# Attention sums as columns: one-column 32-bit products in a bank of scores, with the single key's share added from a list

## What is computed

```python
def sdpa(q, k, v):
    scores = jnp.einsum('bshd,blhd->bhsl', q, k) * scale
    attn = jax.nn.softmax(scores, axis=-1)
    return jnp.einsum('bhsl,blhd->bshd', attn, v)
...
out_img = sdpa(q, k_img, v_img)
out = (out_txt + out_img).reshape(B, S, INNER)
return out @ o_w + o_b
```

## Time and profile before

| what | value |
|---|---|
| median of 3 runs | 1903.29 us (1898.18 to 1903.45) |
| the profiled execution | 1903.73 us, its span 1902.0 us |
| TensorE products, busy | 1733.7 us, 91% |
| VectorE busy | 1397.3 us, 73% |
| GpSimd busy | 1204.3 us, 63% |
| ScalarE busy | 985.9 us, 52% |
| the attention loop | about 231 to 1427 us of the span |

### The profile page before, as it was taken

The page is one execution under the profiler, slowest core; times in us unless marked ns, Lnnn a source line. Parts: engine busy times, 40 slices in busy tenths (PEclk is TensorE's granted clock), DMA queues, the critical chain, the costliest instruction groups (busy, mean ns, idle before and its releaser), DMA issues. The chain is left out here.

```text
span 1902.0 us, 30825 instructions
## 1 busy us (share of the span) xinstructions
PE 1733.7 (91%) x8731; PEld 1541.6 (81%) x8731; DVE 1397.3 (73%) x2577; ACT 985.9 (52%) x1657; POOL 1204.3 (63%) x1053
## 2 busy tenths in 40 slices
PE   7899889999999999999999999999992998699998
PEld 6677778888889889888888898898891886588887
DVE  4444587887887887978878878879772664577776
ACT  3455455565555555655655565556552563244443
POOL 1333588878878888788788798798862231133332
PEclk9999899999999999999999999999996999799999
DMA  3366554566556465554565564564436782133332
GB/s 110 127 239 232 175 164 104 114 123 137 115 118 131 108 117 123 121 120 113 128 132 118 120 134 103 116 128 123 95 92 203 249 267 88 66 109 118 114 115 74
DMA packets 417365, 251.20 MB, mean 132 GB/s; under 512 B 350272, under 2 KB 368832, under 8 KB 415520
## 3 DMA queue, kind: packets, MB, share of 16 engines
q1 hardware_dynamic: 417312, 250.55, 51.5%
HBM read 187.71 MB, written 60.10 MB: 130 GB/s over the span
## 5 line engine op out<-in xcount | busy, mean ns | idle before, releaser
L1341 ACT ACTIVATE p_high<-psum,key_rms 128x448 fp32r<-128x448 f32 x384 | 244.8, 638 | 397.1 <-PE psum L1164 396.9
L1162 PE MATMUL psum<-p_high,c_high 128*128 128x448 f32 (+1 forms) x768 | 287.8, 375 | 48.2 <-DVE p_low L1424 48.2
L1424 DVE TENSOR_TENSOR p_low<-psum,p_high 128x448 fp32r<-128x448 f32 x384 | 236.3, 615 | 96.6 <-ACT psum L1343 95.7
L1162 PE MATMUL psum<-u_high,c_high 128*128 128x448 f32 x768 | 285.9, 372 | 20.2 <-DVE psum L1435 14.1
L1163 PE MATMUL psum<-u_low,c_high 128*128 128x448 f32 x768 | 282.9, 368 | 0.0
L1164 PE MATMUL psum<-u_high,c_low 128*128 128x448 f32 x768 | 281.8, 367 | 0.0
L1164 PE MATMUL psum<-p_high,c_low 128*128 128x448 f32 (+1 forms) x768 | 281.4, 366 | 0.0
L1163 PE MATMUL psum<-p_low,c_high 128*128 128x448 f32 (+1 forms) x768 | 281.0, 366 | 0.0
L1636 POOL TENSOR_TENSOR c_low<-stage,c_high 128x512 fp32r<-128x512 f32 x208 | 274.7, 1321 | 0.0
L1435 DVE COPY psum<-beta_wide 128x448 f32<-128x448 f32 x416 | 259.4, 627 | 20.3 <-DMA beta_wide<-absorbed_biases 4.5
L1630 POOL TENSOR_TENSOR key_rms<-key_ms,minus_half 128x1 f32<-128x1 f32 x209 | 119.4, 571 | 188.4 <-DVE key_ms L1449 183.4
(11 more groups left out here) (245 smaller groups left out, 4077.9 us busy)
## 6 DMA issues: line engine op xcount, KB each, us to landing
stage<-in_ctx SPq DMA_DIRECT2D x210, 256.0 KB, 2.8
averages<-o_raw SPq DMA_DIRECT2D x64, 448.0 KB, 5.2
o_stage<-averages SPq DMA_DIRECT2D x32, 896.0 KB, 5.4
u_raw<-absorbed_queries SPq DMA_DIRECT2D x60, 448.0 KB, 5.5
absorbed_queries<-u_stage SPq DMA_DIRECT2D x14, 1792.0 KB, 6.8
beta_wide<-absorbed_biases SPq DMA_DIRECT2D x32, 448.0 KB, 5.3
recip_wide<-reciprocals SPq DMA_DIRECT2D x32, 448.0 KB, 4.1
p_wide<-probs_by_expert SPq DMA_DIRECT2D x32, 448.0 KB, 3.6
```

Of the source, the lines that this page charges most:

```text
L1162: nc.tensor.matmul(out, high, rhigh, start=start, stop=False, **kw)
L1341: nc.scalar.activation(p_high[:, probs_slot(u), :], src, ACT.Exp, scale=key_rms[:, t:t + 1])
L1424: return nc.vector.tensor_tensor(out, a, b, ALU.subtract)
```

## The change

The products with a matrix of ones are taken out, and with them the split of p_sum, ScalarE's copies and the DMAs that store and load the sums. In their place TensorE's `sums` takes p_sum itself, in 32 bits, as weights: for each of 8 groups of columns (every fourth of a half, 112 of them) one product with a single column of ones. Eight results stand beside each other on 112 partitions, in columns 448 to 455 of a score bank (`sums_of`), which `seed` has set to zero with a small memset. The text's sums of the batch before are taken within `scores` of unit 2, the image's within `scores` of unit 8, ahead of the signal that the scores are done. VectorE takes the reciprocals from PSUM right after the running sum of the same unit. The single key's exponentials are no longer added to p_sum: SyncE lists them on 112 partitions (`list_lone`), and VectorE adds them to the image's sums before the reciprocals. The reciprocals are stored in another order of elements. `norms_first` holds now at step 6 alone; it held at steps 2, 4, 6, 8 and 10.

```diff
@@ seed, on VectorE
+                if u in (TEXT_SUMS, IMAGE_SUMS):
+                    nc.vector.memset(psum[0:TOK, bank_of(u), HALF:HALF + NTOK], 0.0)
@@ scores, on TensorE
+                if u == TEXT_SUMS and has_prev:
+                    last = sums(it - 1, TEXT)
+                if u == IMAGE_SUMS:
+                    last = sums(it, IMAGE)
                 last.then_inc(scores_done, 1)
@@ TensorE
-            def sums(it, s, half, grams):
-
-                n = 4 * it + 2 * s + half
-                pe.wait_ge(sum_split, n + 1 + CREDIT["sum_split"])
-                pe.wait_ge(sum_copied, n + CREDIT["sum_copied"])
-                pe.wait_ge(norm_summed, grams + CREDIT["norm_summed"])
-                nc.tensor.matmul(psum[:, GRAM, 0:HALF], ones_r[:, :], p_sum_high[:, half, :], start=True, stop=False)
-                nc.tensor.matmul(psum[:, GRAM, 0:HALF], ones_r[:, :], p_sum_low[:, half, :], start=False, stop=True)\
-                    .then_inc(sum_wide, 1)
+            def sums(it, s):
+                last = 2 * (LONE if s == 0 else TILES) - 1
+                pe.wait_ge(sum_added, ADDS * it + added(last) + CREDIT["sum_added"])
+                for half in range(2):
+                    parts = p_sum[:, 2 * s + half, :].rearrange("p (n i) -> p i n", i=NTOK // 2)
+                    for i in range(NTOK // 2):
+                        at = NTOK // 2 * half + i
+                        done = nc.tensor.matmul(sums_of(s)[:, at:at + 1], parts[:, i, :], ones[:, 0:1], start=False,
+                                                stop=True, skip_group_check=True)
+                return done
@@ TensorE, after the loop
+                pe.wait_ge(last_zeroed, 1)
+                sums(it - 1, TEXT).then_inc(last_sums, 1)
@@ SyncE
-            def store_sums(it, s):
...
-            def load_sums(it, s):
...
+            def list_lone(it):
+                sp.wait_ge(exp_done, UNITS * it + 2 * LONE + 2 + CREDIT["exp_done"])
+                for half in range(2):
+                    sp.dma_start(lone_cols[:, NTOK // 2 * half:NTOK // 2 * (half + 1)],
+                                 lone_probs[0:1, half, :].rearrange("o (p i) -> o p i", i=NTOK // 2))\
+                        .then_inc(lone_listed, 16)
@@ set_end, on SyncE
+                if has_prev and t == 4:
+                    store_reciprocals(it - 1, TEXT)
                 if has_prev and t == 5:
-                    store_sums(it - 1, TEXT)
-                if has_prev and t == 6:
-                    load_sums(it - 1, TEXT)
-                if has_prev and t == 8:
-                    store_reciprocals(it - 1, TEXT)
-                if has_prev and t == 9:
                     load_reciprocals(it - 1, TEXT)
...
+                if t == 4:
+                    list_lone(it)
+                if t == 7:
+                    store_reciprocals(it, IMAGE)
                 if t == 8:
-                    store_sums(it, IMAGE)
-                if t == 9:
-                    load_sums(it, IMAGE)
-                if t == 10:
-                    store_reciprocals(it, IMAGE)
-                if t == 11:
                     load_reciprocals(it, IMAGE)
@@ VectorE
-            def split_sum(it, s, half):
...
             def reciprocals(it, s):
-                m = 2 * it + s
-                dve.wait_ge(sums_loaded, 16 * (m + 1))
+                m, sums = 2 * it + s, sums_of(s)
+                if s == 0:
+                    dve.wait_ge(lone_listed, 32 * (it + 1) + CREDIT["lone_listed"])
+                    nc.vector.tensor_tensor(sum_cols[:, :], sums, lone_cols[:, :], ALU.add).then_inc(lone_counted, 1)
+                    dve.wait_ge(lone_counted, it + 1)
+                    sums = sum_cols[:, :]
                 dve.wait_ge(recip_stored, 16 * (m - 1) + CREDIT["recip_stored"])
-                nc.vector.reciprocal(recip_cols[:, s, :], sum_cols[:, s, :]).then_inc(recip_ready, 1)
...
+                if u == TEXT_SUMS and has_prev:
+                    reciprocals(it - 1, TEXT)
+                if u == IMAGE_SUMS:
+                    reciprocals(it, IMAGE)
...
-                    norms_first = step % 2 == 0 and (step + 1 in TEXT_SUMS + IMAGE_SUMS or step == 2 * LONE + 2)
+                    norms_first = step == 2 * LONE + 2
```

More of the change, by code:

```diff
@@ L1270, in tail @@
             def tail(it):
-                for step in range(TEXT_SUMS[1] + 1):
+                for step in range(2):
                     carried(it, step)
-                    text_sums(it, step, TILES * it + 1)
+                pe.wait_ge(last_zeroed, 1)
+                sums(it - 1, TEXT).then_inc(last_sums, 1)
             def maxima(it):
@@ L1394, in tail @@
             def tail(it):
-                for step in range(TEXT_SUMS[1] + 2):
+                for step in range(3):
                     carried(it, step)
-                    text_sums(it, step)
             def maxima(it):
@@ L1473, in add @@
                 s, n = int(t >= IMG_TILES), ROWS[t]
+                if t == LONE:
+                    return
                 part, total = probs_of(u)[0:n], p_sum[0:n, 2 * s + half, :]
                 if t in (0, IMG_TILES):
-                    dve.wait_ge(sum_split, 4 * (it - 1) + 2 * s + half + 1 + CREDIT["sum_split"])
-                    added = nc.vector.tensor_copy(total, part)
-                else:
-                    dve.wait_ge(sum_added, UNITS * it + u - 1 + CREDIT["sum_added"])
-                    added = nc.vector.tensor_tensor(total, part, total, ALU.add)
-                added.then_inc(sum_added, 1)
-            def split_sum(it, s, half):
-                last = 2 * (IMG_TILES if s == 0 else TILES) - 2 + half
-                n = 4 * it + 2 * s + half
-                dve.wait_ge(sum_added, UNITS * it + last + 1 + CREDIT["sum_added"])
-                dve.wait_ge(sum_wide, n - 1 + CREDIT["sum_wide"])
-                nc.vector.tensor_copy(p_sum_high[:, half, :], p_sum[:, 2 * s + half, :]).then_inc(sum_high_ready, 1)
-                dve.wait_ge(sum_high_ready, n + 1)
-                sub(p_sum_low[:, half, :], p_sum[:, 2 * s + half, :], p_sum_high[:, half, :].bitcast(F32))\
-                    .then_inc(sum_split, 1)
+                    done = nc.vector.tensor_copy(total, part)
+                else:
+                    dve.wait_ge(sum_added, ADDS * it + added(u) - 2 + CREDIT["sum_added"])
+                    done = nc.vector.tensor_tensor(total, part, total, ALU.add)
+                done.then_inc(sum_added, 1)
             def terms_of_lone(it, half):
@@ L1547, in tail @@
             def tail(it):
-                take(it - 1, UNITS - 1, False)
-                for step in range(TEXT_RECIP + 1):
-                    carried(it, step)
+                take(it - 1, UNITS - 1, True, False)
+                nc.vector.memset(sums_of(TEXT), 0.0).then_inc(last_zeroed, 1)
+                dve.wait_ge(last_sums, 1)
+                reciprocals(it - 1, TEXT)
             def maxima(it):
```

100 lines of the change are left out of this document (28 added, 72 removed).

## The result

The changed kernel takes 1967.1 us in the median of four runs (1961.1 to 1970.2), the kernel before 1901.8 us beside it: 1.034 times as long, 95% interval 1.032 to 1.037. The forecast of 1880 us was wrong, and the time lies outside its range. It is that of rival 2.

The account below looks back on a forecast made before the run. TensorE was taken as the bound, busy 71.09 of 75 us a pass. Gains of 28.5 us over fifteen passes, 1.5 in the first batch and 3.8 after the loop gave 1870; 10 for the clock made 1880 us, range 1862 to 1901.

Parts of the forecast that it names:

- rival 2: Strided weights read at half speed, a `sums` costing 3.2 us: 1916 us, up to 1970 with clock falls; chance 0.13.
- The price of a narrow product: Each one-column 32-bit product on TensorE costs 0.20 us, as in the first layer norm; double as upper end.
- the prediction's own first sign of being wrong: The prediction is wrong if the narrow products on TensorE take over 0.3 us each.
- What goes from TensorE's path: Per pass: eight wide products 1.64 us, waits before averages of units 2, 6, 8 3.77, short delays 0.3; together 5.7.
- the four waits: TensorE's waits per pass, three for p_low and one for unit 8's seed: 1.70, 1.21, 0.55, 1.52 us, 5.0 together.
- The seed wait of unit 8: TensorE's one remaining wait a pass, behind GpSimd's chain: 1.3 to 1.7 us, its cost growing from 1.21 to 1.75.
- A batch where the clock holds: A loop pass: 5.7 gained, 3.2 and 0.5 lost, taken as 1.9 us shorter; 1.0 longer with doubled products.
- The clock: After unit 8's wait and the image's sums, granted clock falls in about 6 of 16 batches, 1.7 us each: 10 us.
- The first batch: The first batch, which has no text sums, gains 1.5 us, between 0 and 4.
- After the loop: Last average's product to stored reciprocals: 6.1 us becomes 2.3, gain 3.8 us, or 2.3 with doubled products.
- the walk of GpSimd's chain: Step-by-step timing of GpSimd's instructions and VectorE's norms up to unit 8's seed: TensorE may start unit 8 at 702.5.
- rival 4: GpSimd becomes the bound, waiting for VectorE's later norms; a pass loses some 1.5 us more: 1903 us; chance 0.06.

Follow-up runs that it names:

- e1_perm: The changed kernel with p_sum's tokens in permuted order, so each narrow product takes 112 contiguous columns as weights; 1884.2 us.
- e4_split: The changed kernel, weights still strided, with each sums' eight products issued as four behind unit 2 (8) and four behind unit 3 (9); 1913.2 us.
- e9_perm_norm: e1_perm with the norm of tile 4 moved behind VectorE's part for unit 5; 1841.6 us.
- e7_norm_behind: The changed kernel with contiguous weights, sums split over two units and the norm of tile 4 moved behind VectorE's part for unit 5; 1836.8 us.
- e12_no_sums_norm: The changed kernel without its narrow products (columns set to one) and with tile 4's norm moved behind VectorE's part for unit 5; 1828.9 us.
- e11_after_norm: The changed kernel, strided and unsplit, with only the norm of tile 4 moved behind VectorE's part for unit 5; 1929.0 us.
- e8_no_sums: The changed kernel without its narrow products, the columns only set to one; 1866.6 us.

## Why the prediction was wrong, point by point

- **The price of a narrow product: the step that failed.** "I take the same price, and double as the upper end." The trace had no strided weights, and the row nearest to it was of contiguous ones. The upper end was the truth: 0.39 us, not 0.20. The range took a price of at most 0.22 and left rival 2 out; the prediction's own first sign of being wrong, over 0.3 us a product, came true. With the price that was taken, e1_perm and its 0.19, the rest of the forecast holds: 1884 us for 1880. The sizes of rival 2 were right as well: 1916 us without falls (e4_split: 1913) and up to 1970 with them (1967). The second is luck in part: it stands for a fall of 3.4 us at every burst, and there were 23 in the loop, of 5.6 us in the mean. What was wrong was its chance, 0.13: no row had a stride in it, so none could speak against a doubling, and I took the nearest row for evidence that it isn't. The Trainium skill's line of 16 bytes (the section named above), which the prediction cites, pointed to the doubling, and I gave it too little weight.
- **What goes from TensorE's path, 5.7 us a batch.** Right. e9_perm_norm has nothing on TensorE but work, 70.73 us. Less its sums, 3.02, that is 67.7. The eight wide products (1.64) and the four waits (5.0) on top make 74.35, and the kernel before takes 74.45: 0.1 for the small delays where I had 0.3. That a wait costs its idle figure and 0.27 us holds too: 70.73 + 1.56 + 0.27 = 72.56 for e1_perm's steady 72.45.
- **The seed wait of unit 8.** Forecast 1.3 to 1.7 us once a batch; 22.1 us in 14 in e1_perm, 1.58 each. In the changed kernel 1.2, since its slower products bring TensorE there later.
- **A batch where the clock holds.** Forecast 1.9 us shorter with contiguous weights: 74.45 - 72.45 = 2.0. With strided ones forecast 1.0 longer: e4_split's steady 75.1 is 0.65 longer.
- **The clock.** Forecast falls at about 6 of 16 image sums, none at the text's, 1.7 us each. e1_perm has 6 in its 15 batches after the first, none at the text's. The mechanism was right, a wait and narrow products in a row (e9_perm_norm, without the wait, has no fall); the count was taken as lying between two other cases, so that it fits is luck, and two of the falls last 6.8 us. In the changed kernel the clock fell at all 15 image sums behind the first and at 8 of the text's, 54 us in all (by e4_split), since the doubled price also made the stretches twice as long. So one wrong term came in twice: as products, 75.1 against 72.45 us a batch or 40 us, and again through the clock.
- **The first batch.** I had a gain of 1.5 us. There the clock of the changed kernel was low for 10.2 us, where the earlier trace rows have 3.4:

```profile
255.00:258.00 3.00, 1.86 (x5) 1.71 (x6) 2.98 (x8) 1.09 (x3) 2.39 (x3) 0.66 0.29 88
258.00:261.00 3.00, 3.00 (x15) 2.89 (x15) 2.55 (x5) 0.00 (x0) 0.14 (x1) 0.50 0.56 138
261.00:264.00 3.00, 3.00 (x12) 2.87 (x13) 0.88 (x3) 1.13 (x2) 0.36 (x1) 0.50 0.80 102
```

  That is 3.4 us more lost than before, if half speed costs half, so the gain wasn't to be had. The fall begins at 255.9 us, 2.6 us ahead of the first narrow product (258.5), so it isn't theirs. e1_perm and e4_split have the same 10.2 us there; in e9_perm_norm and e7_norm_behind, where the first batch's wait of some 1.8 us for unit 8's seed is gone, the clock holds. No kernel measured this term by itself.
- **After the loop.** Forecast 2.3 us from the last average's product to the stored reciprocals, a gain of 3.8, or 2.3 with doubled products. Before, 6.15. The changed kernel, TensorE and then SyncE:

```profile
1492.41 0.37 PE L1158 MATMUL psum<-p_high,c_low 91*128 91x448 f32 x1
1492.62 3.26 PE L1232 MATMUL psum<-ones,p_sum 128*112 128x1 f32 x16
```

```profile
1496.15 0.34 SPq L1014 DMA_DIRECT2D reciprocals<-recip_cols  x1
```

  3.74 us, a gain of 2.4: right for doubled products.
- **GpSimd as the bound (rival 4).** Not reached in the changed kernel, but it lies closer than I put it: 70.3 us a batch, as far as e12_no_sums_norm shows.
- **Two slips in the working.** In the walk of GpSimd's chain 696.5 and 4.74 make 701.24, not 701.35; and the terms named for the low end of the range give about 1865, not 1862. Neither changes the forecast.

The sum: 15 batches of 4.34 us are 65 us; 3.5 us of each are the clock (78.6 against 75.1 in e4_split), and the other 0.8 is what the products cost beyond what the removed waits and wide products gave.

## What to carry to other kernels

When a change reads data in a pattern that no row of the trace has, the nearest row is an end of the range and not its likeliest value; put the chance by what a rule says of the difference, and try the other layout first, since here two rearranged views were worth 83 us. A slow stretch on TensorE made of products of one column is paid twice, once as time and once through the clock: keep it short, and keep it away from waits (with 1.5 us and no wait ahead the clock never fell here). And where several waits are taken away, look for the one that is late next; a move that had been worth 6 us was worth 41, the clock's part included, once the others were gone, and taking out still more work then brought only 13.

## What the runs showed of the hardware

- A load of 112 32-bit weights and its one-column product follow each other in 0.094 us for neighbouring words, 0.098 for every second, 0.195 for every fourth and 0.198 for every eighth (the time of a `sums` over its 16 records at full clock). At half clock it is 0.18 for neighbouring words (2.87 us for 16 in e1_perm) and 0.196 for every fourth (3.14 us in the changed kernel), so there the stride costs a tenth and not the double. VectorE's addition of 448 words from PSUM took the same 0.61 us with steps of one and of four words.
- In e11_after_norm the granted clock fell to half at every one of 30 stretches of 3.1 us of one-column products, not more than 1.5 us behind its end, though both TensorE and its weight loads count as busy throughout (2.80 of 2.80 us in the window 697.40:700.20). Busy time in the profile therefore doesn't tell whether the clock will hold.
- It also fell with no narrow product at all, in 8 of the 15 batches in which waits of 1.35 and 1.59 us ended 3.1 us apart (e8_no_sums), while the four waits a batch of the kernel before, spread out, cost no fall from 300 us on.
